# Second attention, last block: the weighting of the values in two parts, and GpSimd's bias and normalisation behind the last mask

## The reference, cut to what matters

```python
qkv = (layernorm(x) @ attn_w.T + attn_b).reshape(b, n, 16, 24).transpose(0, 2, 1, 3)
q, k, v = jnp.split(qkv, 3, axis=-1)
mask = jnp.arange(n)[:, None] <= jnp.arange(n)[None, :]
scores = jnp.einsum('bhki,bhqi->bhkq', k, q) / math.sqrt(8)
probs = jax.nn.softmax(jnp.where(mask, scores, -10000.0), axis=2)
out = jnp.einsum('bhkq,bhkl->bhql', probs, v).transpose(0, 2, 1, 3).reshape(b, n, 128)
x = x + out @ out_w.T + out_b
```

## Time and profile before

| | us |
|---|---|
| median of 3 runs | 750.63 |
| lowest, highest | 746.75, 751.64 |
| the profiled execution, its own time | 745.6 |
| its span from the first to the last instruction | 743.8 |
| PE busy | 669.7 (90% of the span) |
| DVE, ACT, POOL busy | 492.4, 453.0, 432.0 |
| TensorE's granted clock, mean | 0.979 |

### The profile page before, as it was taken

How to read it: one execution, slowest core, us unless ns; L and a number is a source line. 1 busy time by engine, 2 the same in 40 slices (tenths; PEclk the granted TensorE clock), 3 DMA queues, 4 the chain that set the end, 5 groups by cost and what they waited for, 6 DMA issues and landing times.

```text
span 743.8 us, 13960 instructions
## 1 busy us (share of the span) xinstructions
PE 669.7 (90%) x4706; PEld 471.1 (63%) x4706; DVE 492.4 (66%) x957; ACT 453.0 (61%) x801; POOL 432.0 (58%) x444
## 2 busy tenths in 40 slices
PE   4889996899999989998999999988779899999996
PEld 1445554677877767665555555555446677787784
DVE  6779997657765686466777777766668366776410
ACT  2778876465666655555666666665656466566663
POOL 4545452477787775433444544544555778778772
PEclk9999999899999999999999999999999999999998
DMA  6110320000000003531655656553120000000001
GB/s 188 39 33 28 63 29 2 0 1 1 0 0 0 1 1 115 169 115 44 216 175 181 226 175 203 199 185 135 65 84 18 16 15 14 14 0 16 15 14 29
DMA packets 33028, 52.47 MB, mean 71 GB/s; under 512 B 4560, under 2 KB 9680, under 8 KB 32976
## 3 DMA queue, kind: packets, MB, share of 16 engines
q1 hardware_dynamic: 32784, 51.53, 21.9%
q10 hardware_dynamic: 192, 0.26, 0.1%
HBM read 27.15 MB, written 24.38 MB: 69 GB/s over the span
## 4 chain that ended last, share of the span: by engine, by line
PE 52%; DVE 17%; issue 9%; ACT 7%; POOL 7%; DMA 6%; SPq 1%; DVEq 1%; POOLq 0%; ACTq 0%
PE banks L220 49%; ACT b_prob L1465 3%; DVE b_segment_max L1558 3%; DVE xn L182 3%; DMA b_o_dram<-b_o 3%; POOL f_h_lo L1139 2%; DVE a_mx L651 2%; POOL f_g_lo L1146 2%; ACT a_prob L552 2%; DMA b_den<-b_o_dram 1%; DVE f_hidden L1089 1%; DVE a_prob L665 1%; PE banks L212 1%; POOL b_prob L1668 1%; DVE f_gate L1085 1%
## 5 line engine op out<-in xcount | busy, mean ns | idle before, releaser
L1146 POOL TENSOR_TENSOR f_g_lo<-f_gelu,f_g_hi 128x512 fp32r<-128x512 f32 x128 | 168.3, 1323 | 64.0 <-ACT f_g_hi L1041 63.4
L1040 ACT ACTIVATE f_gelu<-banks,cols 128x512 f32<-128x512 f32 x128 | 88.4, 691 | 134.9 <-PE banks L220 112.9
L1668 POOL TENSOR_SCALAR_AFFINE_SELECT b_prob<-b_prob 128x512 f32<-128x512 f32 x128 | 82.3, 645 | 104.7 <-ACT b_prob L1465 104.4
L1558 DVE TENSOR_REDUCE b_segment_max<-banks 128x6 f32<-128x768 f32 x128 | 116.2, 950 | 34.6 <-PE banks L220 34.4
L1465 ACT ACTIVATE b_prob<-banks 128x768 f32<-128x768 f32 x128 | 102.4, 807 | 56.5 <-PE banks L220 56.5
L220 PE MATMUL banks<-f_g_hi,whi 128*128 128x512 f32 x320 | 131.5, 411 | 4.2 <-POOL f_g_lo L1146 4.2
L220 PE MATMUL banks<-f_g_lo,whi 128*128 128x512 f32 x320 | 127.8, 399 | 0.0
L1139 POOL TENSOR_TENSOR f_h_lo<-f_hidden,f_h_hi 128x512 fp32r<-128x512 f32 x60 | 77.5, 1292 | 61.5 <-DVE f_h_hi L1092 61.5
L220 PE MATMUL banks<-f_h_hi,whi 128*128 128x512 f32 x256 | 106.1, 414 | 4.1 <-POOL f_h_lo L1139 2.4
L220 PE MATMUL banks<-f_h_lo,whi 128*128 128x512 f32 x256 | 102.7, 401 | 0.0
L1041 ACT ACTIVATE f_g_hi<-banks,cols 128x512 fp32r<-128x512 f32 x128 | 87.5, 683 | 0.0
(11 more groups left out here) (124 smaller groups left out, 1048.8 us busy)
## 6 DMA issues: line engine op xcount, KB each, us to landing
f_h_hi<-b_q_dram SPq DMA_DIRECT2D x16, 512.0 KB, 3.9
f_h_lo<-b_k_dram SPq DMA_DIRECT2D x16, 512.0 KB, 5.2
b_o_dram<-b_o SPq DMA_DIRECT2D x8, 1024.0 KB, 4.3
b_q_dram<-b_q_hi SPq DMA_DIRECT2D x16, 256.0 KB, 3.3
b_k_dram<-b_k_hi SPq DMA_DIRECT2D x16, 256.0 KB, 3.6
w_stage<-in_wF SPq DMA_DIRECT2D x8, 352.0 KB, 3.3
b_q_dram<-b_q_lo SPq DMA_DIRECT2D x8, 256.0 KB, 3.3
b_k_dram<-b_k_lo SPq DMA_DIRECT2D x8, 256.0 KB, 3.8
```

The source lines that it names most:

```text
L1040: nc.scalar.activation(gf[c % 2][:, :], z_bank[c % 2], ACT.Gelu, scale=scale).then_inc(s_gf, 1)
L1146: nc.gpsimd.tensor_tensor(lo[:, c, :], gf[c % 2][:, :], hi[:, c, :].bitcast(F32), ALU.subtract).then_inc(s_glo[c % 2], 1)
L1558: nc.vector.reduce_max(seg[:, g, s, 2 * p:2 * p + 2, :], first_pass[:, 2 * p:2 * p + 2, 0:3 * P].rearrange("p b (c k) -> p b c k", c=3), A ...
L1668: nc.gpsimd.affine_select(out=pr, in_=pr, compare_op=ALU.is_ge, fill=0.0, base=0, pattern=[[0, 4], [1, P]], channel_multiplier=-1).then_in ...
```

## The change

Three things, all at block 7:

- The values are weighted in two parts. `pe_values_in_parts` waits for the mask of pair 0, does the four matmuls of its two heads and raises the new semaphore `s_pv0`, then waits for the mask of pair 1 and does the other four. There are as many matmuls as before, in another order. The exponentials of pair 0 wait, from step 2 on, for `s_pv0` of step n - 2 and those of pair 1 for `s_pv`.
- `pool_normalise` of block 6 goes from step 6 of block 7 to behind its last mask.
- `pool_bias` of block 6 goes from step 7 of block 6 to behind that `pool_normalise`.

Beside that the semaphore `shift` is made for the first attention's norm alone, which alone used it.

```diff
+            s_pv0 = sem("b_values_weighted_first_pair")
...
             def pe_values(pe, b, n):
                 g, s = group(n)
+                if is_block(b, LAST):
+                    return pe_values_in_parts(pe, b, n)
...
+            def pe_values_in_parts(pe, b, n):
+                g, s = group(n)
+                if s == 0:
+                    pe.wait_ge(s_oc, GROUPS * b.t + g)
+                for p, done in ((0, s_pv0), (1, s_pv)):
+                    pe.wait_ge(s_ms, UNITS * b.t + PAIRS * n + p + 1)
+                    for kc in range(2):
+                        for j in (2 * p, 2 * p + 1):
+                            pr = prob[n % 2][:, p, :, j % 2, :]
+                            last = mm(o_bank[QUART * j:QUART * j + REP, s * T + kc * P:(s + 1) * T],
+                                      va[b.odd][:, 2 * s + kc, g * GROUPS + j, :],
+                                      pr[:, 1:2, :] if kc else pr[:, 0:3:2, :], start=kc == 0, stop=kc == 1)
+                    last.then_inc(done, 1)
...
             def act_exp(act, b, n, p):
                 act.wait_ge(s_p2, UNITS * b.t + PAIRS * n + p + 1)
-                if p == 0:
+                if is_block(b, LAST) and n > 1:
+                    act.wait_ge(s_pv if p else s_pv0, n - 1 + (STEPS * b.t if p else 0))
+                elif p == 0:
                     wait(act, s_pv, STEPS * b.t + n - 1)
...
             def pool_body(pool, b, before, one, two):
                 nxt = link["next"]
                 for n in range(STEPS):
-                    if before and n == OUT_AT:
+                    if before and one and n == OUT_AT:
                         pool_normalise(pool, b.after(-1))
                     pool_mask(pool, b, n, 0)
...
-                    if one and not two and n == STEPS - 1:
-                        pool_bias(pool, b)
                     pool_mask(pool, b, n, 1)
...
+                if not one:
+                    pool_normalise(pool, b.after(-1))
+                    pool_bias(pool, b.after(-1))
```

More of the change, by code:

```diff
@@ L161, in __init__ @@
                 self.read = sem(f"{layer}_xn_transposed")
-                self.shift = sem(f"{layer}_ln_shift")
+                self.shift = sem(f"{layer}_ln_shift") if layer == "a" else None
             def dve(self, dve, b, first):
```

## The result

The changed kernel took 744.48 us in the median of 11 executions (740.88 to 747.9), the kernel before 748.84 (743.03 to 753.88). The ratio is 0.9944, its 95% interval 0.9917 to 0.9972: 2 to 6 us faster. Within 1% it is, as expected. The profiled execution took 744.48 us, its span is 742.6.

A forecast was written before the change was run, and what follows sets the result against it. No engine is full; a chain from engine to engine was taken to set the time. The terms 0.00 + 0.00 + 0.00 - 0.52 = -0.5 us took the median 750.63 to 750.1 us, range 745.0 to 752.3.

The forecast's parts named there:

- The bias (-0.52): End of block 6: without the bias ahead of the last mask, ACT's copy and the store's issue come 0.52 us sooner.
- Rival A: Output store awaited in block 7: lands in 4.3 us once issued earlier, -1.65 us in all; chance 0.12.
- D's longer store: Wait of ACT's first copy in block 7: store takes longer than 5.46 us, at 6.7 costing +0.7 us; chance 0.12.
- the sum: Whole kernel: two zeros for the parts, zero for the normalisation and -0.52 for the bias, -0.5 us.
- The normalisation (0): Step 6 of block 7: moving it brings values about 1 us sooner, but nothing on the path waits; gain zero.
- The parts (0): Block 7's values in two parts: end at the same distance behind pair 1's mask, exponentials can't profit; zero.
- Rival B: Block 7's values: halves do shorten them, -1.26 us, with the -0.52 making -1.8 us; chance 0.07.
- Rival C: Last gate and projection: the clock's fall doesn't come, -1.24 us, with the 0.52 making -1.8; chance 0.12.
- its variant: End of block 7: no clock fall, but DVE busy to 555.4 delays the addition, -0.6 instead of -1.8 us; chance 0.06.
- Rival F: End of block 7: POOL's late operations shut DVE out; alone costs nothing (750.1), its chance inside the forecast's 0.42.

The follow-up runs named there:

- norm_only: Kernel before with only block 6's normalisation moved behind the last mask of block 7; bias stays in block 6, values weighted at once; ratio 1.0013.
- order_only: Kernel before with block 7's values in the order of the parts, both mask waits ahead of them, exponentials waiting as in the changed kernel; ratio 0.9995.
- bias_only: Kernel before with only block 6's bias moved behind the last mask of block 7; normalisation stays, values weighted at once; ratio 0.9975.
- fill_before: Kernel before with two unread matmuls in each step of block 7, between the waits for the two masks; ratio 0.9957, median 743.94 us against 747.44.

## Why the prediction was wrong

**The bias (-0.52): right on the path, with some luck in the size.** The copy came 0.66 us nearer, the store's issue too (2.69 to 2.03 us behind the landmark), the first copy of block 7 0.48. The store stayed slow: from the last copy's end to the next copy's start it was 5.57 us before and 5.75 after. So 0.14 us more at the copy and 0.18 us lost at the store nearly made up for each other. Rival A didn't come, and of D's longer store only those 0.18 us. What the sum left out is that the move also takes away PE's 1.19 us of idle time at the start of block 7, and that the clock's fall at 3 us came in none of the profiles without it.

**The normalisation (0): right,** by norm_only alone: 1.0013, with an interval of 0.3% to either side. (The 2.1 us that it seems to hold up are 0.91 + 1.29 = 2.2.)

**The parts (0): right on the path, wrong in time.** In block 7 the values end at the old distance behind the second mask; halves that run together take 0.86 us; the looser wait gives nothing (order_only). Rival B is out. This zero is the step that failed: I counted PE's idle time before the values as free, since nobody on the path waited for less of it. What it costs comes afterwards: behind it the granted clock falls to its lower level, 1.2 GHz, and then matmuls on the path take 1.3 to 1.8 times as long. With the first half in it, or with matmuls for nothing, the clock stayed up over the last gate in nine of nine profiles; without, in three of nine.

**Rival C (the clock, -1.24, chance 0.18 with its variant): the mechanism, under-sized and under-weighted.** It held what the zero of the parts left out. I took the one fall in the one profile as the thing at stake and priced it at the gate and the projection. In all five profiles of the kernel before the clock falls in this stretch, one to three times, at three places (bias_only, which weights the values at once too, had one profile without a fall). From the first copy on the kernel before takes 19.14 us in the mean against 17.75 without a fall, 1.4 us lost; the changed kernel 18.70 against 18.20, 0.5 lost. That is -0.9 us, against the 0 of the sum. By the table about 1.0 of the 1.4 us are the falls over the last gate, which don't come with the parts. Ahead of the copy the changed kernel is 0.93 us shorter in the mean (8.52 to 7.59): the bias's 0.5, and about 0.4 us more from the fall at 3 us and from stores of different length, which I can't take apart.

**Rival F (DVE shut out): half of it came.** With the clock up, the addition waited for the layer norm: 0.5 us of the gain lost, not the 1.2 it threatened. The normalisation took 1.71 us instead of 1.29 and the layer norm 3.05 instead of 1.10. Its four instructions are 1.30, 1.31, 0.33 and 0.33 us long: the first ended with the normalisation, the second with the bias, and the other two ran when POOL was done. The Trainium skill's rule (SBUF — State Buffer, section "SBUF: two separate sides": the port pair that DVE and GpSimd share is an exclusive lock) fits these rows.

The sum in block 7 is then -0.5 (bias) - 0.4 (ahead of the copy, the fall at 3 us and the store) - 0.9 (clock from the copy on) + 0.5 (late POOL) = -1.3 us, where the stretch shows -1.4. Another 0.9 us lies behind the transposes in the five profiles of each, with less time at the low clock there. That makes 2.3 us of a measured 4.2, whose interval begins at 2; the whole spans of the ten profiles differ by 2.0 us in the mean. What is open: whether the 0.9 us follow from the change or are chance in ten profiles, and whether the rest is more than the runs' scatter; no run here varied the last layer. So the runs show that the change is faster and, in block 7, why; they don't explain the rest of the 4.2 us. The range was too narrow for a plain reason as well: its lower end rested on the lowest of three runs, 746.75, while 11 runs of the same kernel reach down to 743.03.

## What to carry to other kernels

Where a chain through several engines sets the time, TensorE's idle time is not free even if nothing waits for it to end: look at what the matmuls on the path cost right behind it, and split work so that a part of it runs in the gap. Before a forecast, profile several executions and ask how often and where the clock falls in a stretch, not where it fell in the one that was profiled: what a fall costs went from 0.4 to 1.6 us with its place. And operations moved "out of the way" onto GpSimd's end still have VectorE beside them.

## What the runs showed of the hardware

- Useless matmuls on TensorE can pay: 16 of them made the kernel 0.43% faster (fill_before, interval 0.06 to 0.81%; the unchanged kernel beside itself showed 0.22%, interval -0.11 to 0.55%).
- The scatter of one kernel's executions goes with the granted clock: of the 11 executions of the changed kernel, the one with a mean of 0.988 took 740.88 us, the five with 0.976 or 0.977 took 745.75 to 747.9.
- The same values took 0.86 us at the full clock and 1.50 at the lower (order_only); the gate 1.20 (after) and 2.08 (before).
- Executions of one kernel have their falls at the same few places: 3.2 to 3.4, 13.4 to 13.6 and 22.8 to 23.9 us behind the landmark in the kernel before, 10.2 and 10.4 in the changed one.
